# Filler products on TensorE before the first attention tiles, and the fourth tile's products moved ahead

## What is computed

```python
q  = clip(round(x / s + z), 0, 255)              # fake_quant: (q - z) * s
x  = x + tanh(g_xattn) * (fake_quant(layernorm(x)) @ fake_quant(ctx))
xt = layernorm(x)
scores = softmax(xt @ router_w + router_b) + router_bias   # 4 groups, 2 kept, then 2 experts per token
y  = sum over experts of gate_e * ((silu(xt @ w1 + b1) * (xt @ w2 + b2)) @ w3 + b3)
z  = (silu(xt @ sw1 + sb1) * (xt @ sw2 + sb2)) @ sw3 + sb3
out = x + tanh(g_ffn) * (y + z)
```

## Time and profile before

| | us |
|---|---|
| median of three runs | 322.8 |
| lowest and highest | 322.53 and 323.0 |
| the profiled execution | 322.68 |
| its span, first to last instruction | 321.0 |
| TensorE busy in it | 301.7 (94%) |
| VectorE busy | 197.0 (61%) |
| ScalarE busy | 113.5 (35%) |

### The profile page before, as it was taken

The page is one execution under the profiler, slowest core; times in us unless marked ns, Lnnn a source line. Parts: engine busy times, 40 slices in busy tenths (PEclk is TensorE's granted clock), DMA queues, the critical chain, the costliest instruction groups (busy, mean ns, idle before and its releaser), DMA issues.

```text
span 321.0 us, 4577 instructions
## 1 busy us (share of the span) xinstructions
PE 301.7 (94%) x1804; PEld 149.1 (46%) x1804; DVE 197.0 (61%) x339; ACT 113.5 (35%) x128; POOL 13.9 (4%) x27
## 2 busy tenths in 40 slices
PE   0489999999999999999999999999999999999993
PEld 0234499644544446444444444444444444444441
DVE  4887999969498843765672444648645407135543
ACT  2787598589444495111016300146010000111000
POOL 2100120100002300000000000000000000000000
PEclk9999999999999999999999999999999999999999
DMA  7999708447801560001910006600000000000355
GB/s 257 414 325 344 246 3 244 152 108 198 284 2 21 112 131 2 2 0 37 382 43 0 0 2 202 256 2 0 0 0 0 2 0 3 1 0 2 132 204 195
DMA packets 34311, 34.55 MB, mean 108 GB/s; under 512 B 14789, under 2 KB 29165, under 8 KB 34285
## 3 DMA queue, kind: packets, MB, share of 16 engines
q1 hardware_dynamic: 34276, 34.20, 33.6%
q10 hardware_dynamic: 8, 0.00, 0.0%
HBM read 26.86 MB, written 4.19 MB: 97 GB/s over the span
## 4 chain that ended last, share of the span: by engine, by line
PE 85%; DVE 10%; POOL 1%; DMA 1%; issue 1%; ACT 1%; DVEq 0%
PE PS L1376 26%; PE PS L1197 19%; PE PS L1397 13%; PE PS L1238 13%; PE PS L1132 6%; DVE stats L683 3%; PE PS L1224 2%; PE PS L1210 2%; DVE X L754 2%; PE PS L1139 1%; POOL lnR L394 1%; DMA X<-in_x_dram 1%; DVE wrow L763 1%; PE PS L1245 1%; PE PS L1149 1%
## 5 line engine op out<-in xcount | busy, mean ns | idle before, releaser
L1197 PE MATMUL PS<-areaT,areaW 128*128 128x512 f16 x288 | 62.5, 379 | 0.0
L1197 PEld LDWEIGHTS PS<-areaT,areaW 128*128 128x128 f16 x288 | 28.1, 98 | 33.6
L1238 PE MATMUL PS<-SW,areaH 128*128 128x512 f16 x192 | 41.8, 379 | 0.0
L1397 PE MATMUL PS<-areaW,areaH 128*128 128x512 f16 x192 | 41.8, 379 | 0.0
L1376 PE MATMUL PS<-areaT,area 128*128 128x512 f16 x192 | 41.6, 379 | 0.0
L1376 PE MATMUL PS<-areaT,areaW 128*128 128x512 f16 x192 | 41.6, 379 | 0.0
L627 ACT ACTIVATE SA<-PS,ecol 128x512 f32<-128x512 f32 x8 | 5.5, 687 | 93.0 <-PE PS L1376 93.0
L1132 PE MATMUL PS<-area,areaQ 128*128 128x512 f16 x128 | 32.9, 409 | 3.1 <-DVE area L720 2.2
L1070 DVE SCALAR_TENSOR_TENSOR X<-PS,gcol,X 128x1024 f32<-128x1024 f32 (+1 forms) x18 | 21.0, 1164 | 15.8 <-PE PS L1397 15.8
L1376 PEld LDWEIGHTS PS<-areaT,area 128*128 128x128 f16 x192 | 18.8, 98 | 22.6
L1376 PEld LDWEIGHTS PS<-areaT,areaW 128*128 128x128 f16 x192 | 18.8, 98 | 22.7
(11 more groups left out here) (159 smaller groups left out, 289.2 us busy)
## 6 DMA issues: line engine op xcount, KB each, us to landing
areaT<-in_ctx_dram SPq DMA_DIRECT2D x12, 512.0 KB, 7.4
ring<-in_L_ffn_sw_dram SPq DMA_DIRECT2D x12, 512.0 KB, 6.0
X<-in_x_dram SPq DMA_DIRECT2D x8, 512.0 KB, 7.1
ring<-in_L_ffn_ew_dram SPq DMA_DIRECT2D x4, 1024.0 KB, 7.0
out_dram<-X SPq DMA_DIRECT2D x7, 512.0 KB, 2.6
ring<-in_ctx_dram SPq DMA_DIRECT2D x4, 512.0 KB, 4.1
wrow<-in_L_ffn_ew_dram SPq DMA_DIRECT2D x2, 1024.0 KB, 9.1
rows<-in_L_ffn_eb_dram SPq DMA_DIRECT2D x2, 512.0 KB, 9.0
```

Source lines behind the costliest of these rows:

```text
L1197: last = mm(PS[:, SU_BANK[half * SC + c] + w, lo:hi], SW[:, wp, 2 * c + w, k, :], XT[:, xp, k, tk], start=(k == 0 and n == 0), stop=(k == ...
L1238: last = mm(PS[:, pb + h, :], HT[:, hp, c, i * P:(i + 1) * P], SW3[:, wp, c, hs], start=(c == 0 and n == 0), stop=(c == SC - 1 and n == 2))
L1397: last = mm(PS[:, 2 * (i % 2) + h, :], HE[:, hp, c, i * P:(i + 1) * P], W3S[j][:, wp, c, hs], start=(c == 0 and n == 0), stop=(c == HC - 1 ...
```

## The change

Two things are done to TensorE's program and to no other engine's. A helper `idle_products(n)` issues n products of `zeroh` with `onesh` (128x128x128) into PSUM bank 7, which nobody reads; it is called in six places, 116 products in all. And the products of the fourth tile with blocks 0 to 5 are put behind block 5 of the other three, its block 6 with theirs, so that only its block 7 and its column sums are left at the end. Blocks 0 and 1 of tile 1 also move ahead of block 2 of tile 0.

```diff
@@ -1112,9 +1112,18 @@
             mm = nc.tensor.matmul
+            def idle_products(n):
+                for _ in range(n):
+                    mm(PS[:, 7, 0:P], zeroh[:, :], onesh[:, :], start=True, stop=True)
+
+            pe.wait_ge(consts, 5)
+            idle_products(14)
             pe.wait_ge(ident_rdy, 1)
             pe.wait_ge(sc_wide, 1)
             nc.tensor.transpose(PS[:, 3, 16:20], scx[:, :], idf[0:4, 0:4]).then_inc(sc_T, 1)
+            idle_products(36)
             pe.wait_ge(ident_rdy, 2)
...
@@ -1253,16 +1262,21 @@
             nc.tensor.transpose(PS[:, 3, 20:22], sgx[:, :], idf[0:2, 0:2]).then_inc(sg_T, 1)
+            idle_products(14)
             pe.wait_ge(q1_rdy, 1)
             for k in range(2):
                 pe.wait_ge(q2_rdy, k + 1)
                 products(0, k)
             transpose_q1(1)
+            idle_products(18)
+            pe.wait_ge(q1_rdy, 2)
+            products(1, 0)
+            products(1, 1)
+            idle_products(10)
             pe.wait_ge(q2_rdy, 3)
             products(0, 2)
-            pe.wait_ge(q1_rdy, 2)
-            for k in range(3):
-                products(1, k)
+            products(1, 2)
+            idle_products(24)
             transpose_q1(2)
...
@@ -1277,8 +1291,11 @@
             pe.wait_ge(q2_rdy, 6)
             for i in range(TB - 1):
                 products(i, 5)
+            pe.wait_ge(q1_rdy, TB)
+            for k in range(6):
+                products(TB - 1, k)
             pe.wait_ge(q2_rdy, 7)
-            for i in range(TB - 1):
+            for i in range(TB):
                 products(i, 6)
             pe.wait_ge(q2_rdy, KC)
             for i in range(TB - 1):
@@ -1287,9 +1304,7 @@
                 column_sums(i)
-            pe.wait_ge(q1_rdy, TB)
-            for k in range(KC):
-                products(TB - 1, k)
+            products(TB - 1, KC - 1)
             column_sums(TB - 1)
```

## The result

| | before | changed |
|---|---|---|
| median (us) | 322.78 | 325.88 |
| lowest and highest of six | 322.53 and 323.0, and one at 1127.05 | 325.11 and 327.33 |
| ratio, 95% interval | | 1.0098, 1.0084 to 1.0112 |
| profiled execution, and its span | 322.68, 321.0 | 325.67, 324.0 |

One of the six executions of the kernel before took 1127.05 us; nothing on record says why, and the ratio leaves it out. The changed kernel is slower by 3.1 us. The profiled execution is 3.0 us slower, in span as in time. 325.4 had been forecast, from 324.5 to 327.6.

What follows compares the result with a forecast made beforehand. VectorE's ln2_lo(2), paced from attend(0) and the first column sums, was taken to fix the time; filler zero plus 2.73 us for the fourth tile on 322.68 gave 325.4 us, range 324.5 to 327.6.

Steps and rivals of the forecast that it cites:

- What bounds the kernel: VectorE's finish of ln2_lo(2) at 49.99 us releases TensorE at 50.04; any lateness there reaches the end one for one.
- Part 2: Fourth tile's products ahead: 28 instead of 14 precede the first column sums, which begin at 32.45 instead of 29.72, 2.73 us later.
- Part 1: The 116 filler products run where TensorE waited: cost zero, gain zero.
- step-by-step walk at the low clock: Worst case for the filler: tile 1's transposes 0.6 us late but hidden, tile 2's starting at 24.0 us without a rise.
- The margin at tile 0's transposes: After 36 filler products tile 0's transposes end at 10.96 us, before VectorE's copy at 11.13: 0.15 us late, hidden.
- The place of the rise: TensorE's clock rise comes forward with the filler from 22.4 to 11.6 us, well ahead of the 18.2 needed.
- Rival A: Filler leaves the clock low until 22.4 us, delaying tile 2's transposes and copy: 2.0 us more, 327.4 us; 8%.
- Rival B: Clock falls in TensorE's new pause, 37.2 to 39.5 and 40.7 to 41.7 us: 327.6 us; 4%.
- C: VectorE's stretch from attend(0) to ln2_lo(2) absorbs the delay; its whole 1.00 us idle vanishing gives 324.4 us; 5%.
- D: Shorter tail frees TensorE earlier if VectorE waits for the third and fourth tile: faster, 321.7 us; 4%.

Runs made afterwards that it cites:

- half of the move: Changed kernel with its filler, but only blocks 0 to 2 of the fourth tile (6 products) ahead of the first column sums: 323.84 us, ratio 1.0030.
- exchange: Kernel before plus the filler, with ScalarE's copy of tile 2 put ahead of its quantisation of tile 3: 321.61 us, ratio 0.9969.
- e1: Changed kernel with the fourth tile's products put back where they were, the 116 filler products kept: 322.92 us, ratio 1.0003.
- e2: Kernel before with only the fourth tile's products moved ahead, no filler: 326.04 us, ratio 1.0115.
- e7: Kernel before, no filler, with ScalarE's copy of tile 2 put ahead of its quantisation of tile 3: 321.75 us, ratio 0.9974.
- e8: Kernel before plus filler, ScalarE's tile 2 copy ahead of quantising tile 3, and VectorE's ln2_lo(2) ahead of a shared-weight low half: 321.46 us, ratio 0.9962.
- with the pause filled: Changed kernel plus 36 filler products behind the last column sums and 14 behind the first shared bank's opening: 325.48 us, again 325.33 us.

## Why the prediction was right, point by point

- **What bounds the kernel.** Attend(0) fixes ln2_lo(2), and that fixes all behind 50.04, one for one: held to 0.01 us in the first profile of the changed kernel (17.91 and 265.46 us again), and in both directions, +0.96 (half of the move) and -0.89 us (exchange). The window of VectorE in the earlier trace rows ends at 49.90, 0.09 us before the end of ln2_lo(2) that the prediction takes it to; the sum does not use it.
- **Part 2, 2.73 us.** attend(0) came 2.80 us later, 0.10 of it with the whole front: 2.70. Half of the move came out at 0.99 us as 6 x 0.217 - 0.31 gives it. The 0.31 us that lay in TensorE's wait for S2 were rightly taken off.
- **Part 1, zero.** Right by e1. The step-by-step walk at the low clock was too slow from 12 us on, as the prediction expected: the first product group started at 12.15, tile 1's transposes at 13.56 and not 0.6 us late. The margin at tile 0's transposes was real: 14 products more did cost.
- **The place of the rise.** Forecast at 11.6 us, seen between 11 and 12.15 in the first profile; that close a hit was luck, since other profiles with the same filler have it before 9.7 us. The step took 22.4 us for the rise without filler as if it were a fixed place; e2 and e7 showed it at 19 to 20 us. It did no harm to the sum, since nothing hung on it, and it did harm to the expectation of e7, which hung on it.
- **Rival A** fell. The Trainium skill (TensorE: Matmul & The Clock Gate, Part 4: PE-mode transpose) says that transposes don't count as activity in the same way as products. Between 10.06 and 11.3 us stood nine of them, and the clock was up by 12.15 all the same; filler on both sides may have been enough, so the trace does not decide the rule, but the rule gave no delay.
- **Rival B** is what the prediction mis-sized. It stood as an alternative of 4%, argued away with the clock still full from 318 to 319 us, after one long pause. That was one execution: in the profile of e8 TensorE's last product ends at 313.98, and the clock is at half by 316.2, 2.2 us later.

```profile
316.20:318.00 1.80, 0.00 (x0) 0.00 (x0) 0.00 (x0) 0.00 (x0) 0.00 (x0) 0.50 0.27 94
```

  In move only a pause of 2.18 us was enough. The step that failed is to treat the fall as an event of the whole kernel and not of an execution: it belonged in the sum, with up to 0.9 us on the median. Its price, 2.2 us, is the distance of the slowest executions (327.3 to 327.5 against 327.6 forecast for B); but the falls that rows show cost 0 to 0.8 us, so that this agreement may be chance. Without the fall the median would be near the forecast: with the pause filled it is 325.37 us for 325.4.
- **Rivals C and D** fell: VectorE's stretch absorbed nothing, and attend(3) never waited.

## What to carry to other kernels

Before work is moved ahead because "its data are there", ask who waits for what it is put in front of: here the first tile's sum was wanted at once by the engine that paces the next 20 us, and the fourth tile's not for 10.5 us. Each product put ahead costs its spacing, less what the engine waited there anyway: 2.70 us measured for 2.73, and 0.99 for 0.99. A change that empties a stretch of TensorE further back can also lose it the clock there; filling that pause took away the spread, though not the loss. A profile shows one execution: where the clock rose or fell in it need not hold for the next.

## What the runs showed of the hardware

- Products of zeros with ones into an unused bank bring TensorE's clock up: at 9 to 12 us in the profiles with them, instead of 19 to 23. The 116 of them cost nothing that could be measured (ratio 1.0003, 0.9995 to 1.0012).
- The clock fell from 2.4 to 1.2 GHz half a microsecond after a single stretch of 2.18 us of nothing (move only, granted clock 1.00 up to 40.0 us, 0.50 from 40.5), and in other executions after 2.18 us of nothing, 1.0 us of work and 0.99 us of nothing (0.60 over 41.7 to 46 us), or not at all in the same kernel.
- Where the clock rises differs between executions by some 3 us, with the filler as without.
- The last output transfers take 3.4 to 4.7 us behind VectorE's last instruction, in the same kernel; that alone moves single executions by 1 us.
